# Attention plus mixture-of-experts kernel: routing of a batch from its first 128 tokens, other gates by row products, b2 added in the second expert pass

## The reference

```python
x = x + matmul(fake_quant(layernorm(x)), fake_quant(ctx))     # attention part
h = layernorm(x)
ratio = mean(|h[153:]|) / mean(|h[:153]|)                     # one number per batch
scores = softmax(concat(h, ratio) @ gate_w + gate_b)          # 512 x 3 per batch
top_val, top_idx = top_k(scores, 2); top_val /= sum(top_val)
for i in range(2):
    j = top_idx[:, 0, i]                  # experts: token 0 of each batch decides
    y = act_j(h @ w1[j] + b1[j]) @ w2[j] + b2[j]
    moe += top_val[..., i] * y            # gate values: every token has its own
out = x + moe
```

## Time and profile before

| | |
|---|---|
| device time, median of 3 runs | 399.82 us (399.59 to 400.4) |
| span of the profiled execution | 398.3 us; no separate device time is recorded for it |
| PE busy | 384.2 us, 96% |
| DVE busy | 319.4 us, 80% |
| ACT busy | 194.6 us |
| POOL busy | 75.4 us |
| TensorE clock | full from 28 us on |

### The profile page before, as it was taken

How to read it: one execution, slowest core, us unless ns; L and a number is a source line. 1 busy time by engine, 2 the same in 40 slices (tenths; PEclk the granted TensorE clock), 3 DMA queues, 4 the chain that set the end, 5 groups by cost and what they waited for, 6 DMA issues and landing times.

```text
span 398.3 us, 5246 instructions
## 1 busy us (share of the span) xinstructions
PE 384.2 (96%) x1860; PEld 302.7 (76%) x1860; DVE 319.4 (80%) x529; ACT 194.6 (49%) x253; POOL 75.4 (19%) x94
## 2 busy tenths in 40 slices
PE   1999999999999999999999999999999999999996
PEld 1345656888888888888888888888888888888885
DVE  8689967999599799898899995654997864639972
ACT  3477745274247635372755833344475244424720
POOL 8647500352110001063103001030000010110000
PEclk9999999999999999999999999999999999999999
DMA  8997019719654676728002898965065884550112
GB/s 300 412 410 305 3 50 375 264 21 282 121 105 137 233 229 226 180 39 158 15 0 90 304 291 281 248 118 96 0 209 172 262 275 88 105 106 2 53 53 107
DMA packets 27437, 66.98 MB, mean 168 GB/s; under 512 B 2160, under 2 KB 2192, under 8 KB 27280
## 3 DMA queue, kind: packets, MB, share of 16 engines
q1 hardware_dynamic: 23888, 54.01, 38.8%
q0 software_dynamic: 3456, 12.58, 16.5%
q10 hardware_dynamic: 64, 0.02, 0.0%
HBM read 49.83 MB, written 4.19 MB: 136 GB/s over the span
## 4 chain that ended last, share of the span: by engine, by line
PE 89%; DVE 6%; POOL 1%; issue 1%; ACT 1%; POOLq 0%; ACTq 0%
PE ps L1655 44%; PE ps L1623 38%; PE ps L1415 4%; DVE bn L840 2%; DVE xres L911 2%; PE ps L1449 1%; POOL ctxq L453 1%; PE ps L1403 1%; DVE hT_lo L920 0%; DVE ctxq L858 0%; POOL ctxq L446 0%; DVE q L874 0%; POOL q_rstd L427 0%; DVE q_bias L1147 0%; PE ps L1484 0%
## 5 line engine op out<-in xcount | busy, mean ns | idle before, releaser
L1037 DVE TENSOR_TENSOR w_lo<-raw,w_hi 128x1024 fp32r<-128x1024 f32 x88 | 103.4, 1218 | 2.6 <-ACT w_hi L688 2.4
L688 ACT ACTIVATE w_hi<-raw 128x1024 fp32r<-128x1024 f32 x88 | 87.8, 1052 | 34.5 <-DVE raw L1050 18.0
L1655 PE MATMUL ps<-hT_hi,w_hi 128*128 128x512 f32 x256 | 100.0, 391 | 0.0
L1655 PE MATMUL ps<-hT_lo,w_hi 128*128 128x512 f32 x256 | 99.6, 389 | 0.0
L1655 PE MATMUL ps<-hT_hi,w_lo 128*128 128x512 f32 x256 | 99.6, 389 | 0.0
L1623 PE MATMUL ps<-w_hi,a_hi 128*128 128x512 f32 x224 | 87.4, 390 | 0.0
L1623 PE MATMUL ps<-w_hi,a_lo 128*128 128x512 f32 x224 | 87.2, 389 | 0.0
L1623 PE MATMUL ps<-w_lo,a_hi 128*128 128x512 f32 x224 | 87.1, 389 | 0.0
L776 ACT ACTIVATE act_f<-ps,b1T 128x512 f32<-128x512 f32 x32 | 22.1, 689 | 112.4 <-PE ps L1655 112.4
L523 POOL DMA_DIRECT2D raw<-raw x24 | 21.3, 1038 | 193.0 <-DMA raw<-in_L_ffn_w_dram 137.9
L1655 PEld LDWEIGHTS ps<-hT_hi,w_hi 128*128 128x128 f32 x256 | 48.1, 188 | 10.6 <-issue 0.4
(11 more groups left out here) (155 smaller groups left out, 367.9 us busy)
## 6 DMA issues: line engine op xcount, KB each, us to landing
raw<-in_L_ffn_w_dram SPq DMA_DIRECT2D x64, 512.0 KB, 5.2
raw<-raw POOLq DMA_DIRECT2D x24, 512.0 KB, 6.6
raw<-in_ctx_dram SPq DMA_DIRECT2D x16, 512.0 KB, 11.8
xres<-in_x_dram SPq DMA_DIRECT2D x8, 512.0 KB, 9.7
out_dram<-xres SPq DMA_DIRECT2D x16, 256.0 KB, 4.1
b2row<-in_L_ffn_b_dram SPq DMA_DIRECT2D x4, 512.0 KB, 6.0
gate_rows<-in_L_ffn_gate_w_dram SPq DMA_DIRECT2D x1, 1536.0 KB, 17.7
small<-in_L_xattn_x_scale_dram ACTq DMA_DIRECT2D x2, 0.0 KB
```

The source lines that it names most:

```text
L688: nc.scalar.activation(w_hi[n % SLOTS][:, 2 * c:2 * c + 2, :], region(q)[:, 2 * c:2 * c + 2, :], ACT.Copy).then_inc(w_hi_ready, 1)
L1037: V.tensor_tensor(w_lo[n % SLOTS][:, 2 * c:2 * c + 2, :], region(n % QUARTERS)[:, 2 * c:2 * c + 2, :], w_hi[n % SLOTS][:, 2 * c:2 * c + 2, ...
L1655: last = T.matmul(ps[:, G1_BANK + f % 2, :], w[q % SLOTS][:, k % TT, fs], h[:, k, :], start=n == 0, stop=n == 3 * KT - 1)
```

## The change

1. Batch 0's experts are chosen from the logits of tile 0 alone. PE's `gate_product` for tiles 1 to 3 is gone (48 products), `gate_turn` turns one tile and not four, the copy on ACT is 8x128 and not 8x512.
2. The gate logits of tiles 1 to 3 of batch 0 are now nine `gate_dot` on DVE in pair 0. Those of batch 1 move: tile 0's three to step 5 of pair 1, the other nine to pair 2. There are 21 in all and not 12.
3. `gate_values(b)` moves into step 6 of pair 0 and of pair 2 (from before pair 0, and from the end of pair 1), after a `gate_exp` of the other tiles' scores on ACT at the same step.
4. `h_stats(5..7)` move from pair 0 to steps 0 to 2 of pair 1. POOL's tiny operations of batch 1 move behind the weight sums of pair 0.
5. `bias_add` of both pairs of a batch runs in its second pair: those of pair 0 in steps 0 and 1 of pair 1, those of pair 1 in steps 2 and 3. Pairs 2 and 3 likewise. Since `b2row` holds one row, SP issues the second load of a batch after the w2 loads and after four `bias_add` (`b2_used`).

```diff
+            def load_b2(p, e):
+                if p:
+                    sp.wait_ge(b2_used, TT * p)
+                if p == TOP_K:
+                    sp.wait_ge(hT_ps, B * TT)
+                sp.dma_start(b2row[:], b2[bass.ds(e, 1), :].to_broadcast([P, D])).then_inc(b2_in, 16)
...
                 load_w1(p, 1, e)
-                if p:
-                    sp.wait_ge(b2_used, TT * p)
-                if p == TOP_K:
-                    sp.wait_ge(hT_ps, B * TT)
-                sp.dma_start(b2row[:], b2[bass.ds(e, 1), :].to_broadcast([P, D])).then_inc(b2_in, 16)
+                if p % TOP_K == 0:
+                    load_b2(p, e)
                 load_w1(p, 2, e)
                 load_w1(p, 3, e)
                 for q in range(4):
                     load_w2(p, q, e)
+                if p % TOP_K:
+                    load_b2(p, e)
...
+                            if s == 0 and f == KT - 2:
+                                gate_exp(b, OTHERS, 2 + 2 * b)
...
                 if t == 0:
                     dve.wait_ge(b2_in, 16 * p + 16)
-                    dve.wait_ge(y2_done, 2 * NP * p)
+                    dve.wait_ge(y2_done, 2 * NP * (p // TOP_K * TOP_K + 1))
+                    dve.wait_ge(b2_used, TT * p)
...
             attn_add(1, 2)
-            gate_values(0)
             attn_add(1, 3)
...
-                if p == 1:
-                    gate_dot(3)
-                    gate_dot(4)
...
+                    elif f < 2:
+                        bias_add(p - 1, 2 * f)
+                        bias_add(p - 1, 2 * f + 1)
+                    elif f < 4:
+                        bias_add(p, 2 * f - 4)
+                        bias_add(p, 2 * f - 3)
+                    if p % TOP_K == 0 and f == 5:
+                        dot_scores(p // TOP_K, OTHERS)
+                        score_steps(OTHERS)
+                    if p == 1:
+                        if f < 3:
+                            h_stats(TT + 1 + f)
+                        elif f == 5:
+                            gate_dot(1, 0, 0)
+                            gate_dot(1, 0, 1)
+                            gate_dot(1, 0, 2)
...
             transpose_h(0, 3)
             codes_product(1, 1, 6)
-            gate_product(0, 2)
             transpose_q1(6)
             codes_product(1, 0, 6)
             sum_abs(0)
-            gate_product(0, 3)
             transpose_q1(7)
-            gate_turn(0)
+            gate_turn()
             row_sums(1)
```

More of the change, by code:

```diff
@@ L546, in _ @@
             t4_sum(0)
+            for t in range(TT):
+                h_power(TT + t)
+                h_offset(TT + t)
             t3_sum(1)
@@ L808, in _ @@
                 if p == 1:
[L809 removed]
+                    gate_exp(1, FIRST, 3)
                     split_h(1, 2)
@@ L965, in turned_scores, with dot_scores @@
                 dve.wait_ge(logit_ps, 1)
-                lps = ps[:, TURN_BANK[0], 0:4 * TT].rearrange("p (t e) -> p e t", e=4)
+                lps = ps[:, TURN_BANK[0], 0:4]
                 for e in range(NE):
-                    last = V.tensor_scalar(sc[:, e, :], lps[:, e, :], gbias[:, e:e + 1], None, ALU.add)
+                    last = V.tensor_scalar(sc[:, e, FIRST], lps[:, e:e + 1], gbias[:, e:e + 1], None, ALU.add)
                 then(last)
-            def dot_scores():
-                dve.wait_ge(dots_done, NE * TT)
-                dve.wait_ge(h_rstd_ready, B * TT)
+            def dot_scores(b, cols):
+                first, end = b * TT + cols.start, b * TT + cols.stop
+                dve.wait_ge(dots_done, NE * (end - 1))
+                dve.wait_ge(h_rstd_ready, end)
@@ L980, in dot_scores, with score_steps @@
                 then(last)
[L982 to L986, removed]
+            def score_steps(cols):
+                top, a = sel[:, 0, cols], sel[:, 3, cols]
+                then(V.tensor_tensor(a, sc[:, 0, cols], sc[:, 1, cols], ALU.max))
+                then(V.tensor_tensor(top, a, sc[:, 2, cols], ALU.max))
@@ L987, in score_steps, with rank @@
                 for e in range(NE):
-                    last = V.tensor_tensor(lg[:, e, :], sc[:, e, :], top, ALU.subtract)
+                    last = V.tensor_tensor(lg[:, e, cols], sc[:, e, cols], top, ALU.subtract)
                 last.then_inc(exp_in, 1)
-            def choose_experts(b):
[L993 to L998, removed]
+            def rank(cols, n):
+                top, low, mid, a, c = (sel[:, i, cols] for i in range(5))
+                dve.wait_ge(exp_ready, n)
+                V.tensor_tensor(a, ex[:, 0, cols], ex[:, 1, cols], ALU.max)
+                then(V.tensor_tensor(c, ex[:, 0, cols], ex[:, 1, cols], ALU.min))
+                V.tensor_tensor(low, c, ex[:, 2, cols], ALU.min)
+                then(V.tensor_tensor(top, a, ex[:, 2, cols], ALU.max))
@@ L1000, in choose_experts @@
+            def choose_experts(b):
+                rank(FIRST, 2 * b + 1)
+                top, low = sel[0:1, 0, FIRST], sel[0:1, 1, FIRST]
                 one = lambda i: pick[0:1, i:i + 1]
                 e0 = lambda e: ex[0:1, e, 0:1]
[L1002 to L1005, removed]
+                V.tensor_tensor(one(0), e0(0), top, ALU.is_lt)
+                V.tensor_tensor(one(1), e0(1), top, ALU.is_lt)
+                V.tensor_tensor(one(2), e0(1), low, ALU.is_le)
+                then(V.tensor_tensor(one(3), e0(2), low, ALU.is_le))
@@ L1256, in _ @@
                             s4_sum(p, k - 1)
[L1257 to L1261, removed]
+                    if f == 0 and p > 0:
+                        w_lo_quarter(q + 3)
                     elif f == 2 and p == 0:
@@ L1290, in _ @@
                         router_bias(1)
-                        dot_scores()
-                        score_steps()
+                        dot_scores(1, FIRST)
+                        score_steps(FIRST)
+                    elif p % TOP_K == 0 and f == KT - 2:
+                        gate_values(p // TOP_K)
                 s1_lo(p, 3)
```

139 lines of the change are left out of this document (73 added, 66 removed).

## The result

The changed kernel takes 401.29 us (median of 7 runs, 400.19 to 402.24) against 399.59 for the kernel before in the same series. The medians differ by 1.7 us; the ratio of the two series on record is 1.0051, 95% interval 1.0037 to 1.0064, which stands for 2.0 us. It is slower, where I forecast 0.4 less. A second series gave 1.0061, 1.0047 to 1.0076 (e9). The profiled execution took 401.49 us, span 399.7.

A forecast was written before the change was run, and what follows sets the result against it. PE was taken as the bound, busy 384.2 of 398.3 us. Span 398.3 less 0.9 at the front plus 0.5 waited in pair 1 gave 397.9, that is 399.4 us; range 398.4 to 401.6.

The forecast's parts named there:

- the front: The chain before pair 0: forecast 0.9 us earlier in sum, bounds 0.5 and 1.5.
- the 32 of tiles 1 and 2: Removed gate products beside the ACT and DVE chain before the sum at 49.73: forecast to give nothing.
- What follows on PE to 64.15 is unchanged work: PE from the row sums to pair 0: unchanged work, its awaited terms from ACT and DVE earlier by as much or more.
- Gain 0.7 on PE: Before pair 0: without the last 16 products the row sums start at about 52.25 instead of 52.93.
- where I had 1.55: Expert choice before pair 0: scores added at about 51.35, not 52.90, so w1 loads start 1.55 us sooner.
- w1 loads sooner, 0.2: Earlier w1 loads remove small waits for weights: together 0.1 to 0.3 us, taken as 0.2.
- Pairs 0, 2 and 3 at zero: Work added in these pairs is hidden by spare time and costs zero; PE does not wait there.
- Pair 1, PE waits 0.5: DVE runs late in pair 1 and PE waits 0.5 us, tightest at product 6; bounds 0 and 2.2.
- I took 4.3: Pair 1's b2 row lands 4.3 us after issue, so DVE stands still for 2.3 us.
- where I had 1.45: DVE's lateness in pair 1 left after its idle time at step 7: 1.45 us, carried until PE needs something.
- The first rival, POOL misses its window: Pair 1: POOL's shift is let in too late, PE waits 2.4 us before step 6; 401.3 us, chance 0.25.
- The 1.5 us that I put on top of a span: Profiled span of 398.3 lies 1.5 us below the median of runs, 399.82; the same added to every changed span.

The follow-up runs named there:

- e9: The changed kernel once more, unaltered, on another chip: 401.45 us, ratio 1.0061 to the kernel before.
- e1: The changed kernel with the 32 gate products of tiles 1 and 2 put back on PE, results unused: 399.32 us, ratio 1.000.
- e11: The kernel before without the 48 gate products of tiles 1 to 3, nothing else of the change: 399.57 us, ratio 1.0017.
- e16: The same kernel as e11, run again: the kernel before without the 48 gate products: 400.90 us, ratio 1.003.
- e2: The changed kernel with all 48 gate products put back on PE, logits released behind the last: 399.66 us, ratio 1.0012.
- e10: The changed kernel with six gate products put back, 2 of 16 for each of tiles 1 to 3: 399.74 us, ratio 1.0024.
- e5: e1 plus 12 gate products of tile 3 in PE's wait for ACT ahead of the row sums: 398.91 us, ratio 1.000.
- e3: The kernel before with 28 of the 48 gate products left out (tiles 1 and 2 keep 2 of 16): 400.21 us, ratio 1.0026.
- e6: The kernel before with 42 of the 48 gate products left out (tiles 1 to 3 keep 2 of 16): 399.43 us, ratio 1.001.
- e4: e1 with the additions of the previous pair's b2 all in step 0 of pairs 1 and 3: 399.19 us, ratio 0.9999.
- e8: The changed kernel with the 16 gate products of tile 2 alone put back on PE: 399.05 us, ratio 1.0002.
- e13: The changed kernel with only 12 gate products of tile 3 added, in PE's wait ahead of the row sums: 400.16 us, ratio 1.0017.
- e15: The changed kernel with the previous pair's b2 additions all in step 0 of pairs 1 and 3: 400.90 us, ratio 1.0044.
- e14: e11 with the turn of the logits cut to tile 0, one product set of four: 400.44 us, ratio 1.0027.

## Why the prediction was wrong

**The step that failed** is in the front: "Of the 48 removed products the 32 of tiles 1 and 2 lie beside a chain on ACT and DVE ... I give them nothing", and "What follows on PE to 64.15 is unchanged work". The first puts at nothing a term that was the largest of all; the second is true of the work and not of its speed. I took durations of rows at 2.4 GHz into a kernel in which PE stands still more, and asked only whether the removed work lay on the chain. The cost, in the profiled execution against e1's: 0.40 from the sum to the row sums (3.07, 2.67) and 2.06 from there to pair 0 (13.17, 11.11), 2.5 us in all. No rival had it. The experiments bear it out: with the 32 products back the 2 us are gone (e1), without the 48 the kernel before has the falls too (e11, e16).

**Gain 0.7 on PE.** At full clock 0.53 (e1 against the earlier trace rows: 2.67, 3.20). In the changed kernel the row sums started at 52.21, where I had forecast 52.25, but for a wrong reason: the start ran 0.59 earlier and 0.40 was lost to the clock. Only the distance between two events of one profile shows it. The scores came 2.29 us behind the sum, 3.17 before: 0.9 sooner, where I had 1.55.

**w1 loads sooner, 0.2.** Pair 0 took 81.82 us and not 82.15: 0.33, and the product of 0.50 in its second quarter is gone.

**Pairs 0, 2 and 3 at zero.** Right: no wait of PE in any, DVE 74.50 of 81.82 us in pair 0.

**Pair 1, PE waits 0.5.** Right in place, and in size for this profile, with some luck inside. The row landed 3.6 us after issue (I took 4.3) and DVE stood 1.62 for it (I had 2.3), so that, counted from the start of the pair, the quarter of step 3 began 0.8 sooner than I had it. But POOL's second tile held DVE for about 1.8 and not 0.85:

```profile
182.64 2.24 DVE L1103 SCALAR_TENSOR_TENSOR act_f<-act_f 128x256 f32<-128x256 f32 x1
```

The two cancel: DVE came to step 7 at 194.35, 1.37 later in the pair than before, where I had 1.45. Its lateness came out at product 6, and the pair took 0.54 longer. The size is not fixed, though: with the same code for the pairs it took 85.49 in e2 and e10, as before, and 86.44 in e5. The first rival, POOL misses its window, did not happen: the shift was let in after one addition (0.80) and the tile, 3.40 long, was done at 178.44. The time of that rival, 401.3, was the measured one by chance, and it is only by this rival that the range up to 401.6 takes in the measured time.

**The sum without the clock.** e1 has the whole change but its 32 products: 0.53 and 0.11 at the front, 0.29 in pair 0, less 0.44 in pair 1, is 0.5 below before by these rows; the forecast was 0.4. The medians say 0.1 above, the ratio no difference, with an interval of over 0.5 us either way. The 1.5 us that I put on top of a span were a little short: every timed run on record lies 1.7 to 1.9 above its own span, before and changed alike.

**Shown and open.** Shown: putting products back that nobody reads takes the slowdown away; taking them out of the kernel before brings the falls and a slowdown; the rest of the change, with the products in place, brings no fall and costs 0.9 us at most (e2). Open is part of the size. Long falls cost 2.1 to 2.6 us in e3, e6 and e10, means of runs with against runs without, and short ones 0.6 to 1.0 (e1, e4, e6, e8, e10, e13), and the changed kernel has both kinds as e11 and e16 have. But its runs with a short fall took 400.7 in the mean (3 runs of the first series; 401.1 in e9, 400.6 in e15), where those of e11 took 399.4, of e16 399.7 and of e14 400.3. On one chip (e15 against e14 and e16) the gap is 0.3 to 0.9 us, and pair 1 explains 0.4 of it (85.92 against 85.49 us). On the chip of e9 (two such runs) and e11 it is 1.7, of which pair 1 explains 0.7 (86.22 against 85.49). I have no experiment for the rest. The profiles with a short fall (e6, e13, e14, e15) lie nearer to the changed kernel's times: from the row sums to pair 0 they take 12.44 to 12.75 us, 1.3 to 1.6 more than e1. So it may be the small cost of short falls between runs that is off, by the chance of the start; this is not shown. Nor is why the clock falls in one run of a kernel and not in the next.

## What to carry to other kernels

Work of PE that lies beside the chain isn't free to remove where PE then stands still shortly before the chain needs it: look at how long PE works and pauses ahead of the chain's own products, with the edit and without, and read the row of the granted clock, and how long equal rows take, before looking for a wait. Compare distances between two events within one profile, never absolute starts. Here a few products of no use, placed where PE would wait anyway, kept the clock up and did not lengthen the chain (2.67 us from the sum to the row sums in e1 and e5).

## What the runs showed of the hardware

- The granted clock went to 1.2 GHz though PE's longest pause in the 5 us ahead of the sum over tokens was 0.92 us and PE worked 3.12 of these 5 us; it came back while PE was busy without a break (56 to 57 us). The Trainium skill (TensorE: Matmul & The Clock Gate, Part 1: The HAM clock gate) says that the throttled state is the default and that activity releases it, and tells of a kernel whose clock went to and fro through many small pauses. The falls here agree with that, and show that a single long pause is not needed.
- It is a matter of odds: the clock fell in 3 of 12 runs of one kernel (e3) and 7 of 12 of another (e6), in the nine profiles that have a fall always to 0.50, by the averages mostly for about 3 or 7 us.
- At the start PE works at half speed while the row of the granted clock reads 1.00: 16 transposes took 1.89 us at 9.74 and 1.07 at 33.47 (before), and the next 18 products 6.50 us in one profile and 5.62 in the other.
- A 512 KB row, broadcast to 128 partitions, landed 3.6 us after issue in pair 1 of the changed kernel, behind the last w2 loads; the fastest of a kernel's four such loads took 3.3 to 3.9 us in the kernels that have the change, and the slowest 7.1 to 8.9.
